# A two-layer fp32 transformer block on one core: the software-pipelined step order written anew

## The chip, the cores and the metric

One NeuronCore of one Trainium2 chip runs the kernel. TensorE (PE in the views) multiplies and transposes, VectorE (DVE), ScalarE (ACT) and GpSimd (POOL) work elementwise, SyncE (SP) issues the transfers. The metric is device time in microseconds of one launch.

## The reference, cut to what matters

The input x has 32 batches of 256 rows by 128 columns. Two layers follow each other; each adds an attention and a feed-forward part, both computed from the layer-normalised x.

```python
xn = layernorm(x)
# layer 0: cosine attention + (softmax attention + top-2 of 8 experts)
cos    = clip(l2norm(Q) @ l2norm(K), -0.999, 0.999)      # 16 heads of 8
W      = (1 - arccos(cos) / pi) ** 16
x = x + (W / (sum(W) + 1e-6)) @ V @ Wo + bo
      + softmax(q @ k / sqrt(8)) @ v + sum_top2(gate * (xn @ W_expert + b))
xn = layernorm(x)
# layer 1: causal attention (one head of 128) + FP4 gated MLP (width 352)
x = x + softmax(causal(q1 @ k1 / sqrt(128))) @ v1 @ w_out
      + fp4_linear(silu(fp4_linear(xn, w_gate)) * fp4_linear(xn, w_up), w_down)
```

`fp4_linear` rounds both operands to a grid of 4-bit values in blocks of 16.

## The kernel before, in words

All work on one batch (256 rows, two tiles of 128 partitions) is cut into about 150 small stages, each named by a pair (stage, argument). The list `SCHEDULE` at line 53 holds each of them once, with a lag. Step t of the program walks through the list and runs each stage on batch t + lag, so one step has work of four batches in it: lag 1 (the next batch's layer norm, projections, gate, stacking), lag 0 (scores), lag -1 (power, values, end of layer 0, start of layer 1) and lag -2 (end of the MLP). Steps t = -1 to 33 are run; 28 of them in a hardware loop of two steps a turn. Every engine walks through the same list and issues, in this order, only its own part of each stage. There is no planner at run time: an engine waits on semaphores for its inputs and for buffers, and everything behind a waiting instruction waits too.

The stages that the prediction speaks of, with what they issue in a step:

- `c` (8): PE makes the cosines of two heads in `psS`; DVE clips them into `curve` (L852). `sq` (4): POOL squares 2048 columns of `curve` into `root` (L500). `ln` (4): ACT logarithm of `root`. `sigm` (4): ACT sigmoid of `root`. `mul` (4): `curve` times `root`, arguments 0 and 2 on POOL (L503), 1 and 3 on DVE (L848). `arctan`, `wln`, `wexp` (4 each): ACT on `curve`. `pvw` (8): PE, values under these weights (L1199). `oC`, `oF`: ACT copies the sums out of `psV`; `finc`, `finf`: PE transposes them, DVE divides (L876 to L887).
- `m` (8): PE scores, DVE row maxima (L858). `maxT`: DVE splits the maxima, PE transposes, ACT copies `mT`. `e` (8): PE scores less the maxima, ACT exponentials `prob`. `pvf` (8): PE, values.
- `xnT`: DVE normalises, PE transposes, ACT copies `xnT`. `proj` (2): PE projects (L1004), ACT copies cosine q, k, v, DVE copies the softmax ones and the gate's (L769 to L774). `norm`: ACT squares, DVE sums (L779). `guess`: ACT, first guess of the inverse norms. `newton`: DVE refines them into `rn` (L791 to L793). `unit`: POOL multiplies q and k by `rn` (L514). `high` (4): ACT, high halves into `stk`; arguments 0 and 1 are the softmax k and q, 2 and 3 the cosine ones, which wait for `unit`. `stack` (4): POOL, low halves (L520). `stackT` (4): PE transposes, DVE copies (L844). `choose` (6), `gmax`, `gexp`: gate.
- `wo`, `ln1`, `rstd1`, `xn1T`, `quantx` (9 DVE steps of FP4 rounding), `p1`, `s1`, `s1e`, `p1T`, `o1`, `w1` (DVE L940), `xqT`, `gu` (2, PE L1167, ACT sigmoid `h`), `hmul` (2, DVE L946 and L948), `quanth` (9 DVE steps on 128x704, L409 to L425), `hT`, `down`: layer 1. `fadd`: POOL. `table` (2): ACT loads a table of functions (L563, L636).

Two lists are derived from `SCHEDULE`: `MISC` gives all small PE products their places in two PSUM banks in turn, `SCORES` does so for `c`, `m`, `e` in two slots of `psS`. A PE product waits until the one before it in its bank or slot has been read. So an order changes also which stage waits for which buffer. SP's queue has only `load` (lag 1) and `down`'s store (lag -2).

```python
for stage, arg, lag in SCHEDULE:
    if not isinstance(t, int) or 0 <= t + lag < B:
        run(stage, arg, t + lag, (parity + lag) % 2, t)
```

```python
if kind < 2:                       # high, on ACT
    act.wait_ge(s_stkq, due(s_stkq, b))
```

Of the kernel before, what the change touches and what calls it, by code (L numbers as in the profile page):

```python
# [1225 lines left out]
```

## Time and profile before

| what | value |
|---|---|
| median of 3 runs | 2045.9 us (2045.52 to 2048.73) |
| profiled execution, own time | 2050.03 us |
| its span | 2048.2 us |
| ACT busy | 1875.9 us (92%) |
| DVE busy | 1790.3 us (87%) |
| PE busy | 1625.1 us (79%) |
| POOL busy | 1062.5 us (52%) |
| mean granted TensorE clock | 0.924 |
| DMA | 11.21 MB, mean 5 GB/s |

Busy is the time in which at least one instruction of the engine ran. Instructions of one engine overlap a little at their ends, so the distance from one start to the next (below called pitch) can be shorter than a duration. A wait is shown in brackets behind a row of the timeline as the idle time and the instruction that ended it.

### The profile page before, as it was taken

How to read it: one execution, taken by the hardware profiler on the slowest of the kernel's cores; microseconds unless marked ns; L12 is line 12 of the kernel's file. 1: busy time of each engine (PE TensorE's matmuls, PEld its weight loads, DVE VectorE, ACT ScalarE, POOL GpSimd, SP SyncE). 2: the span in 40 equal slices, each digit the busy share in tenths (PEclk: the TensorE clock that was granted, in tenths of full speed). 3: DMA queues.
4: the chain of work that ended last, by engine and by line, in shares of the span. 5: the costliest groups of instructions: out<-in, count | busy, mean ns of one | idle time of the engine just before them, and what ended most of it. 6: DMA issues, size and time to landing. Idle time of an engine off the chain costs nothing.

```text
span 2048.2 us, 39684 instructions
## 1 busy us (share of the span) xinstructions
PE 1625.1 (79%) x12405; PEld 796.0 (39%) x12405; DVE 1790.3 (87%) x4071; ACT 1875.9 (92%) x2144; POOL 1062.5 (52%) x448
## 2 busy tenths in 40 slices
PE   2678788888888888888888888888888888887865
PEld 1233444433444443344444334444433444443433
DVE  5778989999998999999899999989999998998844
ACT  2399999999999999999999999999999999999991
POOL 1455555456555545655554565555456555545520
PEclk9979999999999999999999999999999999999875
DMA  1000000000000000000000000000000000000000
GB/s 41 4 4 1 6 6 0 5 6 5 6 5 6 0 5 6 5 6 5 6 0 5 6 5 6 5 6 0 5 6 5 6 5 6 0 5 7 4 4 6
DMA packets 21059, 11.21 MB, mean 5 GB/s; under 512 B 1431, under 2 KB 20953, under 8 KB 20956
## 3 DMA queue, kind: packets, MB, share of 16 engines
q1 hardware_dynamic: 20956, 10.20, 1.7%
q14 instruction: 83, 0.68, 0.1%
q8 instruction: 20, 0.33, 0.1%
...
## 4 chain that ended last, share of the span: by engine, by line
ACT 40%; DVE 23%; issue 22%; PE 13%; POOL 1%; DVEq 1%; ACTq 1%; SPq 0%; DMA 0%; POOLq 0%
ACT curve L532 21%; ACT root L532 7%; ACT prob L532 3%; PE psM L1167 3%; DVE nmax L858 3%; DVE curve L848 3%; PE psM L1004 2%; ACT L563 2%; ACT L636 1%; PE psV L1199 1%; DVE h L421 1%; ACT hqT L532 1%; POOL qk L514 1%; PE psM L1151 1%; DVE hqT L417 1%
## 5 line engine op out<-in xcount | busy, mean ns | idle before, releaser
L532 ACT ACTIVATE curve<-curve 128x2048 f32<-128x2048 f32 x384 | 717.7, 1902 | 4.8 <-POOL curve L503 3.4
L500 POOL TENSOR_TENSOR root<-curve 128x2048 f32<-128x2048 f32 x128 | 460.1, 3600 | 426.1 <-DVE curve L852 425.9
L532 ACT ACTIVATE root<-root 128x2048 f32<-128x2048 f32 x256 | 484.4, 1905 | 8.1 <-POOL root L500 7.8
L503 POOL TENSOR_TENSOR curve<-curve,root 128x2048 f32<-128x2048 f32 x64 | 348.8, 5452 | 93.3 <-ACT root L532 93.3
L852 DVE TENSOR_SCALAR curve<-psS 128x1024 f32<-128x1024 f32 x256 | 306.0, 1216 | 25.3 <-PE psS L1035 19.1
L858 DVE TENSOR_REDUCE nmax<-psS 128x4 f32<-128x1024 f32 x256 | 308.8, 1214 | 7.2 <-PE psS L1044 6.9
L1199 PE MATMUL psV<-prob,vf 128*32 128x256 f32 x2048 | 270.8, 425 | 3.9 <-ACT prob L532 0.6
L532 ACT ACTIVATE prob<-psS 128x1024 f32<-128x1024 f32 x256 | 261.3, 1021 | 11.8 <-PE psS L1065 11.0
L1199 PE MATMUL psV<-curve,vc 128*32 128x256 f32 x2048 | 225.4, 408 | 40.0 <-ACT curve L532 36.3
L520 POOL TENSOR_TENSOR stk<-qk,stk 128x512 f16<-128x512 f32 x128 | 168.4, 1325 | 155.3 <-ACT stk L532 155.3
L848 DVE TENSOR_TENSOR curve<-curve,root 128x2048 f32<-128x2048 f32 x64 | 177.7, 2777 | 5.6 <-ACT root L532 5.6
L832 DVE SCALAR_TENSOR_TENSOR acc<-psM,comb,acc 128x128 f32<-128x128 f32 x512 | 142.1, 344 | 27.0 <-PE psM L1012 25.4
L1167 PE MATMUL psM<-wguT,xqT 128*128 128x352 f32 x256 | 126.6, 623 | 42.0 <-ACT xqT L532 23.0
L1199 PEld LDWEIGHTS psV<-curve,vc 128*32 128x32 f32 x2048 | 96.4, 114 | 144.4 <-issue 111.1
L1012 PE MATMUL psM<-we,xnT 128*128 128x512 f32 x256 | 151.2, 674 | 0.0
L1199 PEld LDWEIGHTS psV<-prob,vf 128*32 128x32 f32 x2048 | 94.9, 118 | 141.8 <-issue 75.9
L1063 PE MATMUL psS<-stkT 32*128 32x256 f16 x1024 | 129.6, 276 | 2.0 <-ACT prob L532 1.6
L1065 PE MATMUL psS<-mT,onesb 32*128 32x256 bf16 x1024 | 127.3, 271 | 0.0
L1044 PE MATMUL psS<-stkT 32*128 32x256 f16 x1024 | 108.8, 294 | 3.5 <-DVE nmax L858 2.4
L1023 PE MATMUL psM<-ident,stk 128*128 128x128 f16 x1024 | 76.7, 225 | 36.9 <-DVE stkT L844 32.0
L514 POOL TENSOR_TENSOR qk<-qk,rn 128x512 f32<-128x512 f32 x32 | 34.4, 1073 | 136.3 <-DVE rn L793 136.3
L1035 PE MATMUL psS<-stkT 32*128 32x256 f16 x1024 | 83.7, 292 | 20.1 <-DVE curve L852 15.1
...
## 6 DMA issues: line engine op xcount, KB each, us to landing
...
```

Source lines behind the costliest of these rows:

```text
L500: nc.gpsimd.tensor_tensor(root[:, two], curve[:, p, two], curve[:, p, two], ALU.mult).then_inc(s_sq, 1)
L503: nc.gpsimd.tensor_tensor(curve[:, p, two], curve[:, p, two], root[:, two], ALU.mult).then_inc(s_half[0], 1)
L520: nc.gpsimd.tensor_tensor(lo, src, hi, ALU.subtract).then_inc(s_stk, 1)
L532: return nc.scalar.activation(out, in_, func, **kw)
L832: nc.vector.scalar_tensor_tensor(acc[:, p, j, :], bank[:, (e % 4) * D:(e % 4 + 1) * D], comb[:, p, j, e:e + 1], acc[:, p, j, :], ALU.mult, ...
L848: nc.vector.tensor_tensor(curve[:, p, two], curve[:, p, two], root[:, two], ALU.mult).then_inc(s_half[1], 1)
L852: nc.vector.tensor_scalar(curve[:, p, arg * UC:(arg + 1) * UC], psS[:, slot_of(stage, arg), :, :, :].rearrange("p a k q -> p (a k q)"), CO ...
L858: nc.vector.tensor_reduce(nmax[:, :, 2 * arg:2 * arg + 2].rearrange("p j a -> p a j"), psS[:, slot_of(stage, arg), :, :, :], AX.X, ALU.max ...
L1012: mm(bank[:, :], xnT[:, j * P:(j + 1) * P], we[:, 4 * arg:4 * arg + 4, :].rearrange("p e f -> p (e f)"), start=False, stop=True).then_inc( ...
L1063: mm(psS[:, slot, a, kt, :], stkT[rows(hh), 3, g, kt * P:(kt + 1) * P], stkT[rows(hh), 2, g, :], start=True, stop=False)
L1167: ins = mm(bank[:, 0:I], xqT[:, arg * P:(arg + 1) * P], wguT[:, m, :], start=True, stop=True)
L1199: ins = mm(psV[rows(hh), kind, half, :], head_window(v, p, kt, head_at(g, hh)), w[:, a, kt, :], start=(g % 2 == 0 and kt == 0), stop=(g % ...
```

## The change

Only the list `SCHEDULE` is replaced, by one with the same stages in another order; every instruction is the same. Some lags differ: `c` 1, 2 and 3 and `sq` 0 move from lag 0 to lag 1, `m` 3 from 1 to 0, `o1` from -2 to -1, `hmul` 1 from -1 to -2 (that is, over the boundary of a step). The core of it:

```diff
-    ("table", 0, -1), ("wln", 0, -1), ("c", 1, 0), ("sq", 0, 0), ("fadd", 0, -1), ("pvf", 7, -1), ("oF", 0, -1),
...
-    ("ln", 0, 0), ("m", 6, 0), ("experts", 1, 0), ("pvw", 3, -1), ("sq", 1, 0), ("sq", 2, 0), ("m", 7, 0),
-    ("pvw", 4, -1), ("sq", 3, 0), ("rstd0", 0, 1), ("stack", 0, 1), ("pvw", 5, -1), ("quanth", 1, -2), ("load", 0, 1),
-    ("unit", 0, 1), ("ln", 1, 0), ("oC", 0, -1), ("pvw", 6, -1), ("pvw", 7, -1), ("xnT", 0, 1), ("maxT", 0, 0),
-    ("quanth", 2, -2), ("quanth", 3, -2), ("c", 6, 0), ("c", 7, 0), ("proj", 0, 1), ("finc", 0, -1), ("stack", 1, 1),
-    ("ln", 2, 0), ("e", 0, 0), ("proj", 1, 1), ("norm", 0, 1), ("ocT", 0, -1), ("e", 1, 0), ("high", 0, 1),
-    ("w1", 0, -2), ("wo", 0, -1), ("stack", 2, 1), ("e", 2, 0), ("pvf", 0, 0), ("pvf", 1, 0), ("pvf", 2, 0),
-    ("ln1", 0, -1), ("ln", 3, 0), ("quanth", 4, -2), ("rstd1", 0, -1), ("xn1T", 0, -1), ("guess", 0, 1),
-    ("gexp", 0, 1), ("quantx", 0, -1), ("quanth", 5, -2), ("gmax", 0, 1), ("stack", 3, 1), ("quanth", 6, -2),
-    ("newton", 0, 1), ("e", 3, 0), ("quantx", 1, -1), ("choose", 0, 1), ("p1", 0, -1), ("high", 1, 1), ("e", 4, 0),
-    ("high", 2, 1), ("quanth", 7, -2), ("s1", 0, -1), ("choose", 1, 1), ("e", 5, 0), ("quantx", 2, -1), ("pvf", 3, 0),
-    ("s1e", 0, -1), ("e", 6, 0), ("high", 3, 1), ("quanth", 8, -2), ("quantx", 3, -1), ("residual", 0, 1),
...
-    ("pvf", 6, 0), ("down", 0, -2), ("mul", 2, 0), ("arctan", 1, 0), ("p1T", 0, -1), ("choose", 4, 1), ("mul", 3, 0),
-    ("arctan", 2, 0), ("gu", 1, -1), ("arctan", 3, 0), ("choose", 5, 1), ("hmul", 1, -1),
+    ("table", 0, -1), ("c", 4, 0), ("hmul", 1, -2), ("pvf", 7, -1), ("wln", 0, -1), ("wexp", 0, -1), ("m", 3, 0),
+    ("wln", 1, -1), ("ln0", 0, 1), ("wln", 2, -1), ("sq", 1, 0), ("quanth", 0, -2), ("wexp", 1, -1), ("c", 5, 0),
...
+    ("w1", 0, -2), ("pvw", 3, -1), ("m", 7, 0), ("rstd0", 0, 1), ("ln", 0, 0), ("ln", 1, 0), ("pvw", 4, -1),
+    ("sq", 2, 0), ("pvw", 5, -1), ("pvw", 6, -1), ("xnT", 0, 1), ("maxT", 0, 0), ("pvw", 7, -1), ("oC", 0, -1),
+    ("c", 7, 0), ("proj", 0, 1), ("oF", 0, -1), ("sq", 3, 0), ("finc", 0, -1), ("finf", 0, -1), ("ln", 2, 0),
+    ("e", 0, 0), ("quanth", 3, -2), ("proj", 1, 1), ("norm", 0, 1), ("ocT", 0, -1), ("e", 1, 0), ("gmax", 0, 1),
+    ("e", 2, 0), ("quanth", 4, -2), ("wo", 0, -1), ("guess", 0, 1), ("high", 0, 1), ("quanth", 5, -2), ("ln1", 0, -1),
+    ("pvf", 0, 0), ("fadd", 0, -1), ("unit", 0, 1), ("load", 0, 1), ("e", 3, 0), ("quanth", 6, -2), ("pvf", 1, 0),
+    ("e", 4, 0), ("rstd1", 0, -1), ("high", 1, 1), ("pvf", 2, 0), ("e", 5, 0), ("xn1T", 0, -1), ("pvf", 3, 0),
+    ("quanth", 7, -2), ("quantx", 0, -1), ("quantx", 1, -1), ("quanth", 8, -2), ("quantx", 2, -1), ("newton", 0, 1),
+    ("gexp", 0, 1), ("stack", 0, 1), ("e", 6, 0), ("quantx", 3, -1), ("choose", 0, 1), ("quantx", 4, -1),
+    ("p1", 0, -1), ("stack", 1, 1), ("s1", 0, -1), ("choose", 1, 1), ("high", 2, 1), ("quantx", 5, -1), ("pvf", 4, 0),
+    ("stackT", 0, 1), ("choose", 2, 1), ("ln", 3, 0), ("s1e", 0, -1), ("e", 7, 0), ("quantx", 6, -1),
...
+    ("sigm", 1, 0), ("hT", 1, -2), ("xqT", 0, -1), ("sigm", 2, 0), ("c", 0, 1), ("mul", 0, 0), ("choose", 5, 1),
+    ("mul", 1, 0), ("mul", 2, 0), ("rs1", 0, -1), ("gu", 0, -1), ("sigm", 3, 0), ("sq", 0, 1), ("hmul", 0, -1),
+    ("pvf", 6, 0), ("c", 1, 1), ("down", 0, -2), ("c", 2, 1), ("arctan", 0, 0), ("arctan", 1, 0), ("o1", 0, -1),
+    ("arctan", 2, 0), ("gu", 1, -1), ("mul", 3, 0), ("arctan", 3, 0), ("c", 3, 1),
```

## Rows read from the trace of the kernel before

**Rows 1.** Busy us (xcount) of PE, PEld, DVE, ACT, POOL, granted clock, DMA: 300 to 900.

```profile
300.00:900.00 600.00, 494.70 (x3888) 243.29 (x3886) 553.40 (x1256) 585.39 (x664) 332.45 (x131) 0.95 0.02 5
```

**Rows 2.** The instructions of line 563, the table load that opens a step on ACT.

```profile
L563 ACT ACT_TABLE_LOAD  x32: 1283/1283/1283, 127.4 to 1981.7; - x32
```

**Rows 3.** Timeline of ACT over one period, from the middle of the run.

```profile
1013.37 0.46 ACT L532 ACTIVATE h<-psM 128x352 f32<-128x352 f32 x1 [1.00 <-PE psM L1167]
...
1024.87 1.91 ACT L532 ACTIVATE curve<-curve 128x2048 f32<-128x2048 f32 x1
1026.69 0.58 ACT L532 ACTIVATE oFs<-psV 128x512 f32<-128x512 f32 x1
...
1043.96 0.58 ACT L532 ACTIVATE oCs<-psV 128x512 f32<-128x512 f32 x1
1044.44 0.37 ACT L532 ACTIVATE xnT<-psM 128x256 f32<-128x256 f32 x1
...
1048.12 1.03 ACT L532 ACTIVATE prob<-psS 128x1024 f32<-128x1024 f32 x1
1049.02 0.40 ACT L532 ACTIVATE qk<-psM 128x256 f32<-128x256 f32 x1
...
1059.38 0.64 ACT L532 ACTIVATE stk<-qk 128x512 f16<-128x512 f32 x1
...
1104.33 0.37 ACT L532 ACTIVATE xnT<-psM 128x256 f32<-128x256 f32 x1
```

**Rows 4.** Timeline of DVE over the same period.

```profile
1011.50 2.88 DVE L848 TENSOR_TENSOR curve<-curve,root 128x2048 f32<-128x2048 f32 x1
...
1030.63 0.34 DVE L885 RECIPROCAL rsF<-psM 128x32 f32<-128x32 f32 x1
1031.02 0.42 DVE L887 TENSOR_TENSOR of<-psM,rsF 128x256 f32<-128x256 f32 x1
...
1047.07 0.41 DVE L769 TENSOR_TENSOR qk<-psM,wfb 128x256 f32<-128x256 f32 x1
...
1048.27 0.42 DVE L880 TENSOR_TENSOR oc<-psM,rsC 128x256 f32<-128x256 f32 x1
1049.71 0.42 DVE L769 TENSOR_TENSOR qk<-psM,wfb 128x256 f32<-128x256 f32 x1 [1.02 <-PE psM L1004]
...
1051.30 0.61 DVE L940 SCALAR_TENSOR_TENSOR x<-psM,rs,x 128x128 f32<-128x128 f32 x2
...
1057.54 0.23 DVE L793 SCALAR_TENSOR_TENSOR rn<-rnt,rn 128x64 f32<-128x64 f32 x1
```

**Rows 5.** The instructions of six lines; durations in ns, least, median, longest.

```profile
L417 DVE TENSOR_SCALAR hqT<-h x32: 494/718/726, 215.8 to 2034.4; 128x704 uint32<-128x704 uint32 x32
L423 DVE SCALAR_TENSOR_TENSOR h<-hqT,h x32: 882/1440/1444, 220.9 to 2036.4; 128x704 f32<-128x704 f32 x32
L425 DVE TENSOR_TENSOR h<-h,qa x32: 826/1359/1368, 223.9 to 2037.4; 128x704 f32<-128x704 f32 x32
L848 DVE TENSOR_TENSOR curve<-curve,root x64: 2276/2885/4499, 115.3 to 1975.6; 128x2048 f32<-128x2048 f32 x64
L503 POOL TENSOR_TENSOR curve<-curve,root x64: 4524/5441/6610, 112.1 to 1970.5; 128x2048 f32<-128x2048 f32 x64
L500 POOL TENSOR_TENSOR root<-curve x128: 3593/3600/3605, 67.8 to 1945.0; 128x2048 f32<-128x2048 f32 x128
```

**Rows 6.** Timeline of POOL over the same period.

```profile
1012.44 6.37 POOL L503 TENSOR_TENSOR curve<-curve,root 128x2048 f32<-128x2048 f32 x1 [0.20 <-ACT root L532]
...
1057.92 1.07 POOL L514 TENSOR_TENSOR qk<-qk,rn 128x512 f32<-128x512 f32 x1 [4.40 <-DVE rn L793]
```

**Rows 7.** Timeline of PE over the same period.

```profile
1010.62 2.71 PE L1167 MATMUL psM<-wguT,xqT 128*128 128x352 f32 x4 [0.30 <-ACT xqT L532]
...
1048.75 0.93 PE L1004 MATMUL psM<-wf,xnT 128*128 128x392 f32 x2
```

**Rows 8.** The view of rows 1 for 1010 to 1015 us.

```profile
1010.00:1015.00 5.00, 4.70 (x16) 1.73 (x12) 4.70 (x5) 4.00 (x6) 4.79 (x2) 0.50 0.00 0
```

More of the change, by code:

```diff
@@ L69 @@
-    ("quantx", 4, -1), ("choose", 2, 1), ("pvf", 4, 0), ("e", 7, 0), ("quantx", 5, -1), ("table", 1, 0),
-    ("stackT", 0, 1), ("stackT", 1, 1), ("sigm", 0, 0), ("quantx", 6, -1), ("stackT", 2, 1), ("quantx", 7, -1),
-    ("hT", 0, -2), ("choose", 3, 1), ("sigm", 1, 0), ("quantx", 8, -1), ("m", 0, 1), ("stackT", 3, 1), ("mul", 0, 0),
-    ("m", 1, 1), ("hT", 1, -2), ("xqT", 0, -1), ("m", 2, 1), ("mul", 1, 0), ("sigm", 2, 0), ("gu", 0, -1),
-    ("pvf", 5, 0), ("hmul", 0, -1), ("rs1", 0, -1), ("m", 3, 1), ("arctan", 0, 0), ("sigm", 3, 0), ("c", 0, 1),
@@ L74 @@
-    ("pvf", 6, 0), ("down", 0, -2), ("mul", 2, 0), ("arctan", 1, 0), ("p1T", 0, -1), ("choose", 4, 1), ("mul", 3, 0),
-    ("arctan", 2, 0), ("gu", 1, -1), ("arctan", 3, 0), ("choose", 5, 1), ("hmul", 1, -1),
+    ("table", 0, -1), ("c", 4, 0), ("hmul", 1, -2), ("pvf", 7, -1), ("wln", 0, -1), ("wexp", 0, -1), ("m", 3, 0),
+    ("wln", 1, -1), ("ln0", 0, 1), ("wln", 2, -1), ("sq", 1, 0), ("quanth", 0, -2), ("wexp", 1, -1), ("c", 5, 0),
+    ("quanth", 1, -2), ("wln", 3, -1), ("experts", 0, 0), ("m", 4, 0), ("pvw", 0, -1), ("wexp", 2, -1), ("m", 5, 0),
@@ new lines @@
+    ("experts", 1, 0), ("pvw", 1, -1), ("quanth", 2, -2), ("pvw", 2, -1), ("wexp", 3, -1), ("m", 6, 0), ("c", 6, 0),
+    ("w1", 0, -2), ("pvw", 3, -1), ("m", 7, 0), ("rstd0", 0, 1), ("ln", 0, 0), ("ln", 1, 0), ("pvw", 4, -1),
+    ("sq", 2, 0), ("pvw", 5, -1), ("pvw", 6, -1), ("xnT", 0, 1), ("maxT", 0, 0), ("pvw", 7, -1), ("oC", 0, -1),
+    ("c", 7, 0), ("proj", 0, 1), ("oF", 0, -1), ("sq", 3, 0), ("finc", 0, -1), ("finf", 0, -1), ("ln", 2, 0),
+    ("e", 0, 0), ("quanth", 3, -2), ("proj", 1, 1), ("norm", 0, 1), ("ocT", 0, -1), ("e", 1, 0), ("gmax", 0, 1),
@@ new lines @@
+    ("p1", 0, -1), ("stack", 1, 1), ("s1", 0, -1), ("choose", 1, 1), ("high", 2, 1), ("quantx", 5, -1), ("pvf", 4, 0),
+    ("stackT", 0, 1), ("choose", 2, 1), ("ln", 3, 0), ("s1e", 0, -1), ("e", 7, 0), ("quantx", 6, -1),
+    ("residual", 0, 1), ("table", 1, 0), ("choose", 3, 1), ("stack", 2, 1), ("high", 3, 1), ("quantx", 7, -1),
+    ("pvf", 5, 0), ("quantx", 8, -1), ("stackT", 1, 1), ("choose", 4, 1), ("stackT", 2, 1), ("sigm", 0, 0),
+    ("m", 0, 1), ("m", 1, 1), ("hT", 0, -2), ("stack", 3, 1), ("p1T", 0, -1), ("stackT", 3, 1), ("m", 2, 1),
```

3 lines of the change are left out of this document (removed).

## The prediction

> **What bounds the kernel now.** I read first the busy time by stretch: in the long middle of the run ACT is busy for 585.4 of 600 us and DVE for 553.4 [rows 1]. A reordering takes no work away, so at most the 2.4% in which ACT rests are there to be won, and a new wait of ACT costs its full length, since ACT has almost nothing to make it up with. Then the table loads: a step opens with one, 32 of them from 127.4 to 1981.7 us, so a period is 1854.3 / 31 = 59.8 us [rows 2], ahead of it lie 127 us of filling and behind it 66 us of draining. Third the timeline of ACT over one period: its instructions follow each other at 1.82 us for 2048 columns (1024.87 to 1026.69) and 0.90 for `prob` (1048.12 to 1049.02), with one clear wait of 1.00 us, for the first product of `gu` [rows 3].
>
> I cut a period at two points of ACT: X, the start of the copy `xnT` (1044.44), and H, the start of `high` 2 (1059.38), the first that needs `unit`. From X to H it is 14.94 us now, from H to the next X (1104.33) 44.95 [rows 3]. Both stretches hold in the new order too, and a circle runs through them: X lets PE project, DVE copies, finishes the norms, POOL multiplies, and only then may ACT do H; from H on ACT works in order until X. The period can't be shorter than this circle.
>
> **The change, from H to X.** By the two lists, ACT has two `e`, `oC` and `oF` less in this stretch than now and one `ln` more: -2 x 0.90 - 2 x 0.48 (1043.96 to 1044.44) + 1.82 = -0.94 us [rows 3]. `wexp` 0 now stands right behind `wln` 0, whose output it reads, so it can't begin before that one has ended: 1.91 in place of 1.82, some +0.1 [rows 3]. The wait at `gu` 0 stays: again only `sigm` 2 stands between the copy `xqT` and it, and the products take 2.71 us at a granted clock of 0.50 [rows 7, 8]. I follow the other inputs by their places: mul 2, mul 3, `hT`, `stackT`, the `wexp` for `pvw` come out in time, some by less than 1 us. So 44.95 - 0.94 + 0.1 = 44.1 us.
>
> The moved lags cost nothing of their own: `c` 1 to 3 and `sq` 0 are the same work a little sooner, `hmul` 1 finds its input (`gu` 1) ready because `mul` 3, `c` 3 and `c` 4 (some 4.5 us of DVE) stand between, and `o1` is copied out of PSUM in ACT's order a step sooner, beside `p1T` as before. SP's queue has the same two stages; `load` 0 passes no store, and the input is needed a whole step later. If that cover were gone, `ln0` would be late first, and it has 12 us to X.
>
> **From X to H.** ACT's own work here grows by two `e`, `oC` and `oF` less one `ln`, to about 14.6 us of pitches [rows 3], but DVE is longer, and it is behind the same X:
>
> - X to the second `proj` on DVE: 5.27 us now (1044.44 to 1049.71), with `finc` between the two [rows 3, 4]. Now `finf` is there too, and since both copies leave the same two banks, the last product of `proj` 1 must wait until DVE has read `finf`. X to the first copy 2.63, copy and `finc` 1.62 (1047.07 to 1048.69), `finf` 0.81 (1030.63 to 1031.44), the product 0.93, two handovers of 0.05: 6.1 [rows 4, 7]. `quanth` 3 lies in the shadow of that product, but may begin late (below): I take 6.3.
> - From there to the end of `newton`: 8.06 us now (1049.71 to 1057.77) [rows 4]. `w1` goes away, 0.61 and its wait of 0.1 [rows 4]. `quanth` 7 and 8 and `quantx` 1 and 2 come in ahead of it. `quanth` 7 and 8 have a median of 1.44 and 1.36, but a least of 0.88 and 0.83 [rows 5]. The difference is a wait for POOL: now they run beside POOL's `unit` and `stack`. In the new order `unit` waits for `newton`, which is behind them, and nothing else is left for POOL, so I take the least: 1.71, less 0.1 of overlap. For the same reason `quanth` 4 goes from 0.72 to 0.49 [rows 5]. The two small ones are 0.3. Sum: 8.06 - 0.7 + 1.6 - 0.2 + 0.3 = 9.1.
> - `newton` to the end of `unit`: 1.22 us now (1057.77 to 1058.99) [rows 4, 6]. `quantx` 3, with two inputs in SBUF, comes directly behind `newton` and is ahead of `unit` by the 0.15 that the semaphore takes; I add 0.2.
>
> 6.3 + 9.1 + 1.4 = 16.8 us, against 14.94. ACT stands before `high` 2 (and a little before `ln1`, which is also behind more DVE work) and loses what it now has in small waits and more. DVE in turn has rested before `proj` 0.
>
> **The sum.** 16.8 + 44.1 = 60.9 us a period against 59.8: +1.1. A period pays this when it has both lag 1 and lag -2 work, t = 2 to 30, so 29 times: +32 us. The filling and draining chains hold the same steps; I see 1 or 2 us either way and take zero. The profiled execution's own 2050.0 us becomes 2082, and the median, 4.1 lower, 2045.9 + 32 = 2078 us.
>
> **A row and a rule.** DVE's `mul` at 1011.50 took 2.88 us where the least is 2.28, and POOL's `mul` began at 1012.44, took 6.37, where the least is 4.52 [rows 4 to 6]. That is 0.6 of DVE waiting, until POOL's previous `mul` ended, and then 1.9 of POOL waiting, until DVE's ended at 1014.38: 1012.44 + 1.94 + 4.43 = 1018.81. They don't share, they take turns. The Trainium skill says so on the page SBUF — State Buffer, section "SBUF: two separate sides": whichever of the two starts first holds the shared pair of ports for its whole instruction, and the other blocks. The trace agrees with it by these numbers.
>
> **The rivals.**
>
> *A, the turn lost (slower still).* In the new order POOL has `sq` 0 directly behind `mul` 2, and DVE comes to `mul` 3 at about H + 18.7, while by the same durations `mul` 2 ends at H + 19.5, having waited for `mul` 1 [rows 5]. If DVE is there first it goes ahead of `sq` 0 and ends at 21.8, in time for `arctan` 3 at 22.1. If it comes over 0.8 us later, `sq` holds the ports for 3.60 us [rows 5] and `arctan` 3 is late by about 3.3 us: +4.4 a period, +128 us, 2174; in some periods only, by that share. By the rule of the Trainium skill, SBUF — State Buffer, section "Who interferes with whom", each such miss costs the whole rest of the other instruction; the forecast's sum has the good turn.
>
> *B, the clock moves.* The products of `gu` 0 ran at half clock and those of the circle, `proj`, `finc`, `finf`, `e`, did not [rows 7, 8]. With PE's pauses elsewhere, the half clock can fall on the circle: two products of the 0.93 kind lie on it [rows 7], so half the clock costs about 1 us, as much as at `gu` 0, +2.1 a period, +61 us: 2107.
>
> *C, the other side: faster.* The half clock leaves `gu` 0 and doesn't come to the circle: up to the 1.00 us of that wait is gone [rows 3]. With the short end of the circle too (6.0, 8.9 and 1.22: 16.1) a period is 59.2, -0.6: -17 us, 2029. It decides against the forecast from the point where the circle is shorter than 15.7 us with the wait at its present size, or 16.7 without it. For it speaks only that the clock moved in and out in the old order too; against, that DVE's added steps are there in the list.
>
> *D, nothing shows.* `quanth` and the rest lie in DVE's slack (46.6 us in 600) [rows 1] and the wait before `high` 2 only takes the place of the small ones that ACT has now: period as before, 2046. This needs the two errors of C at half size.
>
> **How the numbers follow.** Forecast 0.50 (a period longer by 0.4 to 1.9), A 0.12, B 0.12, C 0.16, D 0.10. That leaves a measured difference under 0.2% (4 us, about what a measurement of this kernel can tell from none) to D: faster 0.16, same 0.10, slower 0.74. For the range: the low end takes C's half, a period of -0.3 us: 2037; the high end must take B's whole and the costs at which I took the least: `quanth` 7 and 8 at their medians are +1.1 a period, +32 over the forecast, 2110, and a few turns lost on top, 2118.
>
> **What the profile would show.** Right: the two table loads of a period about 60.9 us apart; ACT with a wait of 1 to 2 us before a `stk` instruction, ended by POOL L514, in nearly every period; POOL L514 with a wait for DVE L793 longer than now; L423 and L425 on `h` near 0.88 and 0.83; DVE resting before L769. A: a wait of ACT before a `curve` activation, ended by DVE L848, of about 3 us, and L848 over 5 us. B: L1004 and L1080 longer, PEclk 0.50 in their stretch. C: no wait of `h` for L1167 and a wait before `stk` below 1 us. The prediction is wrong at its root if ACT waits nowhere for L514: then I mistook which engine is last at H. It is wrong in size if the stretch from H to X isn't near 44.1, which would mean a wait that I passed over when I followed the places.

## The result

The changed kernel takes 2094.95 us (median of 4, 2090.68 to 2098.91), the one before 2047.32 (4 runs, 2045.52 to 2050.22): ratio 1.0227, 95% interval 1.0214 to 1.0239, so 47.6 us slower. 2078 was predicted, with a range of 2037 to 2118. The direction and the place are right; 15.6 us of the loss are missing.

Two lines of the page of the changed kernel, the busy time and the granted clock in 40 slices. ACT's work is the same as before, its share lower; the granted clock is under 0.9 in more slices, its mean is 0.876 where it was 0.924.

```profile
span 2093.7 us, 39627 instructions
PE 1728.5 (83%) x12405; PEld 830.3 (40%) x12405; DVE 1778.0 (85%) x4071; ACT 1882.2 (90%) x2144; POOL 1122.6 (54%) x448
...
PEclk9678889989889898888998888998988998988976
```

The view of [rows 1], and the table loads of [rows 2], now of the changed kernel. In the middle ACT is busy for 571.5 of 600 us instead of 585.4. The loads lie 1904.7 / 31 = 61.44 us apart instead of 59.82: 1904.7 - 1854.3 = +50.4 over the 31 periods. Less 2.2 ahead of the first and 2.7 behind the last (63.8 us instead of 66.5), this makes 45.5, and the two profiled executions differ by 45.5 (2095.52 and 2050.03).

```profile
300.00:900.00 600.00, 518.53 (x3783) 248.66 (x3779) 531.45 (x1224) 571.49 (x643) 338.59 (x125) 0.89 0.02 5
```

```profile
L563 ACT ACT_TABLE_LOAD  x32: 1283/1283/1283, 125.2 to 2029.9; - x32
```

The timeline of ACT over one ordinary period (compare [rows 3]). X is at 1004.85, H at 1021.70, the next X at 1065.83: 16.85 and 44.13 us, where 16.8 and 44.1 were forecast. (That the first agrees so well is luck in part, see below.)

```profile
1004.85 0.36 ACT L532 ACTIVATE xnT<-psM 128x256 f32<-128x256 f32 x1
1007.15 0.38 ACT L532 ACTIVATE qk<-psM 128x256 f32<-128x256 f32 x1 [0.55 <-PE psM L1004]
...
1021.70 0.63 ACT L532 ACTIVATE stk<-qk 128x512 f16<-128x512 f32 x1 [0.17 <-POOL qk L514]
...
1035.94 0.46 ACT L532 ACTIVATE h<-psM 128x352 f32<-128x352 f32 x1 [1.01 <-PE psM L1167]
...
1046.04 1.28 ACT L563 ACT_TABLE_LOAD   x1
...
1065.83 0.36 ACT L532 ACTIVATE xnT<-psM 128x256 f32<-128x256 f32 x1
```

DVE and POOL in the same period (compare [rows 4, 6]). The second projection's copy on DVE is at X + 7.04, `newton` ends 8.46 later (1020.35), `unit` ends 1.28 after that (1021.63): the circle. L423 and L425 (`quanth` 7 and 8) take 0.88 each.

```profile
1007.81 0.42 DVE L769 TENSOR_TENSOR qk<-psM,wfb 128x256 f32<-128x256 f32 x1 [0.27 <-PE psM L1004]
...
1010.20 1.77 DVE L415 SCALAR_TENSOR_TENSOR h<-h,qr 128x704 f32<-128x704 f32 x1
1011.89 0.41 DVE L769 TENSOR_TENSOR qk<-psM,wfb 128x256 f32<-128x256 f32 x1
...
1017.38 0.88 DVE L423 SCALAR_TENSOR_TENSOR h<-hqT,h 128x704 f32<-128x704 f32 x1
...
1018.71 0.88 DVE L425 TENSOR_TENSOR h<-h,qa 128x704 f32<-128x704 f32 x1
...
1020.13 0.22 DVE L793 SCALAR_TENSOR_TENSOR rn<-rnt,rn 128x64 f32<-128x64 f32 x1
...
1041.08 2.38 DVE L848 TENSOR_TENSOR curve<-curve,root 128x2048 f32<-128x2048 f32 x1
```

```profile
1007.62 3.60 POOL L500 TENSOR_TENSOR root<-curve 128x2048 f32<-128x2048 f32 x1 [14.34 <-DVE curve L852]
...
1020.52 1.11 POOL L514 TENSOR_TENSOR qk<-qk,rn 128x512 f32<-128x512 f32 x1 [7.96 <-DVE rn L793]
...
1035.01 6.30 POOL L503 TENSOR_TENSOR curve<-curve,root 128x2048 f32<-128x2048 f32 x1 [0.74 <-ACT root L532]
```

But not all periods are like this one. These are means over the same 25 periods of each trace (X number 5 to 29 to the next X), read off the timelines of ACT:

| kernel | X to H | H to X | period |
|---|---|---|---|
| before | 14.94 | 44.80 | 59.74 |
| changed | 17.22 | 44.23 | 61.44 |

In the changed kernel every fifth period from X = 818.61 on has 19.4 us from X to H. Here is PE's timeline just behind that X, and the window view there. The clock is 0.72, the products of the maxima and of `pvw` 7 are late (1.01 and 1.92 us, where they take 0.61 and 1.06 at X = 1004.85, at a clock of 1.00), and `curve` on DVE, ahead of the projection's copy, waited 3.60 us (2.11 in an ordinary period, at most 1.3 before). The projection's own products run at full clock (0.91).

```profile
819.15 1.01 PE L1055 MATMUL psM<-identb,mstk 128*128 128x128 bf16 x8 [0.65 <-DVE mstk L868]
820.09 1.92 PE L1199 MATMUL psV<-curve,vc 128*32 128x256 f32 x8
821.94 0.53 PE L1035 MATMUL psS<-stkT 32*128 32x256 f16 x4
822.40 0.91 PE L1004 MATMUL psM<-w0T,xnT 128*128 128x384 f32 x2
```

```profile
818.00:824.00 6.00, 5.29 (x27) 2.39 (x27) 2.12 (x6) 2.99 (x7) 0.09 (x1) 0.72 0.00 0
```

Two of DVE's waits for TensorE between 300 and 1800 us have grown, from 14.3 to 70.1 and from 12.2 to 42.6 us. Most of the first belongs to the order itself: DVE now comes to the clip of `c` 7 with nothing else to do and waits 2.11 us for its product in ordinary periods too. The second, for the experts' products, is the one that goes when the clock is up again (10.0 us in experiment 10, where the first is still 62.4):

```profile
DVE curve L852 <- PE psS L1035: 70.1, 46, 3.7
...
DVE acc L832 <- PE psM L1012: 42.6, 54, 2.0
```

This second wait also reaches ordinary periods. Rows of DVE and PE ahead of X = 1004.85: the experts' product takes 2.08 us, DVE waits for it, and so it ends its split of the maxima (L868) at 1004.21, 0.64 before X. In experiment 10 it ends 1.23 before X (997.52, X = 998.75), and the projection, whose products take the same time in both, comes 0.59 sooner behind X. The same holds period by period, in the 25 of the changed kernel and the 25 of experiment 10: where DVE waits 0.2 or 0.7 us for the experts in the 25 us ahead of X, the second projection's copy comes at X + 6.4; where it waits 1.5 to 1.8, at X + 6.9 to 7.1; where it waits 2.4 to 3.2, at X + 8.2 to 9.7.

```profile
990.87 1.90 DVE L832 SCALAR_TENSOR_TENSOR acc<-psM,comb,acc 128x128 f32<-128x128 f32 x7 [0.99 <-PE psM L1012]
...
1003.91 0.30 DVE L868 TENSOR_TENSOR mstk<-nres,mstk 128x32 bf16<-128x32 f32 x1
```

```profile
988.75 2.08 PE L1012 MATMUL psM<-we,xnT 128*128 128x512 f32 x2
```

### The profile page after: what moved, and what is told of

Same layout as the page of the kernel before. It is cut to its first block, busy times and chain, and to the rows that moved or that the text cites. A ratio compares the mean times of both kernels' runs of the same rounds, so it can differ in the third digit from the quotient of the medians.

```text
span 2093.7 us, 39627 instructions
## 1 busy us (share of the span) xinstructions
PE 1728.5 (83%) x12405; PEld 830.3 (40%) x12405; DVE 1778.0 (85%) x4071; ACT 1882.2 (90%) x2144; POOL 1122.6 (54%) x448
## 4 chain that ended last, share of the span: by engine, by line
DVE 32%; PE 31%; ACT 17%; issue 16%; POOL 2%; DVEq 1%; SPq 0%; ACTq 0%; DMA 0%; POOLq 0%
PE psM L1012 8%; PE psV L1199 6%; ACT curve L532 5%; ACT root L532 4%; DVE curve L852 4%; PE psM L1167 4%; DVE curve L848 3%; DVE nmax L858 3%; PE psM L1004 2%; PE psM L1011 2%; ACT L636 2%; DVE h L415 2%; PE psS L1044 2%; ACT prob L532 2%; PE psS L1035 2%
## 5 line engine op out<-in xcount | busy, mean ns | idle before, releaser
L500 POOL TENSOR_TENSOR root<-curve 128x2048 f32<-128x2048 f32 x128 | 523.1, 4097 | 482.0 <-DVE curve L852 480.3
L1199 PE MATMUL psV<-prob,vf 128*32 128x256 f32 x2048 | 286.7, 403 | 0.0
L532 ACT ACTIVATE prob<-psS 128x1024 f32<-128x1024 f32 x256 | 254.6, 1020 | 13.7 <-PE psS L1065 9.0
L1199 PE MATMUL psV<-curve,vc 128*32 128x256 f32 x2048 | 237.6, 413 | 29.4 <-ACT curve L532 22.5
L1012 PE MATMUL psM<-we,xnT 128*128 128x512 f32 x256 | 206.0, 898 | 1.2 <-issue 1.2
L514 POOL TENSOR_TENSOR qk<-qk,rn 128x512 f32<-128x512 f32 x32 | 35.5, 1108 | 285.9 <-DVE rn L793 285.9
L520 POOL TENSOR_TENSOR stk<-qk,stk 128x512 f16<-128x512 f32 x128 | 149.9, 1181 | 71.0 <-ACT stk L532 71.0
L848 DVE TENSOR_TENSOR curve<-curve,root 128x2048 f32<-128x2048 f32 x64 | 162.7, 2542 | 6.2 <-ACT root L532 6.2
L1167 PE MATMUL psM<-wguT,xqT 128*128 128x352 f32 x256 | 132.9, 636 | 38.5 <-ACT o1T L532 33.3
L1023 PE MATMUL psM<-ident,stk 128*128 128x128 f16 x1024 | 84.0, 237 | 37.8 <-ACT hqT L532 28.7
L1065 PE MATMUL psS<-mT,onesb 32*128 32x256 bf16 x1024 | 112.4, 268 | 0.0
```

What stands on the lines that cost most here:

```text
L500: nc.gpsimd.tensor_tensor(root[:, two], curve[:, p, two], curve[:, p, two], ALU.mult).then_inc(s_sq, 1)
L520: nc.gpsimd.tensor_tensor(lo, src, hi, ALU.subtract).then_inc(s_stk, 1)
L532: return nc.scalar.activation(out, in_, func, **kw)
L848: nc.vector.tensor_tensor(curve[:, p, two], curve[:, p, two], root[:, two], ALU.mult).then_inc(s_half[1], 1)
L1012: mm(bank[:, :], xnT[:, j * P:(j + 1) * P], we[:, 4 * arg:4 * arg + 4, :].rearrange("p e f -> p (e f)"), start=False, stop=True).then_inc( ...
L1167: ins = mm(bank[:, 0:I], xqT[:, arg * P:(arg + 1) * P], wguT[:, m, :], start=True, stop=True)
```

## The experiments

Two theories. *Circle*: the new order puts `quanth` 7 and 8 and `quantx` 1 and 2 ahead of `newton`, and a period is as long as the way X, projection, DVE, `newton`, `unit`, H and ACT's work back to X. *Clock*: the loss, or what of it the circle doesn't give, comes from TensorE being granted half its clock (1.2 in place of 2.4 GHz) in other places. List edits are shown cut to the entries that move. Three kernels add products that change no value; this is said where they come.

**1. Undo the late `newton` alone**, in the changed kernel.

```diff
     ("xn1T", 0, -1),
+    ("newton", 0, 1),
     ("pvf", 3, 0), ("quanth", 7, -2), ("quantx", 0, -1), ("quantx", 1, -1), ("quanth", 8, -2), ("quantx", 2, -1),
-    ("newton", 0, 1),
```

> The changed order with one stage moved back: newton directly behind xn1T, so ahead of quanth 7, quantx 0 and 1, quanth 8 and quantx 2. Nothing that TensorE does moves. Circle theory (DVE's work ahead of newton makes ScalarE wait at high 2): newton ends 2.3 us sooner, ScalarE's own work becomes last in the stretch from xnT to high 2, which falls from 16.9 to about 15.6 us, while quanth 7 and 8 grow from 0.88 to about 1.4 us beside GpSimd, where nobody waits for them: period 61.4 to about 60.1, time about 2057 us (2045 to 2065). Rival, half clock: the periods whose proj runs at half clock carry the loss, DVE's order does not; then the time stays within 10 us of 2095. Rival, banks: the products of proj 1 waiting for finf's bank carry it; then it stays near 2095 too.

2156.72 us, ratio 1.0535 [1.0514, 1.0555]: slower still. At best, X to H fell to 15.98, no further: there `unit` had ended 1.59 us before H (X = 1029.69, `unit` at 1044.08, H at 1045.67), so this is ACT's own way from X to H in the new order, its small waits included. H to X rose from 44.2 to 45.2 or more in most periods, since ACT's exponential of layer 1 now waits for DVE's maxima (17.2 us in 23 waits between 300 and 1800), and to 47.5 to 49.5 in nine of the periods, where a turn is lost. The row of ACT at this H, then rows of DVE, POOL and ACT in a period with a lost turn: DVE's `mul` 3 came at 1128.54, 0.86 after POOL's `mul` 2 had ended at 1127.68, and by then POOL had begun the square (1127.63). The square took its 3.60, DVE's instruction ended at 1133.38, and ACT's arctangent had stood for 2.52.

```profile
1045.67 0.62 ACT L532 ACTIVATE stk<-qk 128x512 f16<-128x512 f32 x1
```

```profile
1128.54 4.84 DVE L848 TENSOR_TENSOR curve<-curve,root 128x2048 f32<-128x2048 f32 x1
```

```profile
1121.61 6.07 POOL L503 TENSOR_TENSOR curve<-curve,root 128x2048 f32<-128x2048 f32 x1 [0.57 <-ACT root L532]
1127.63 3.60 POOL L500 TENSOR_TENSOR root<-curve 128x2048 f32<-128x2048 f32 x1
```

```profile
1133.41 1.91 ACT L532 ACTIVATE curve<-curve 128x2048 f32<-128x2048 f32 x1 [2.52 <-DVE curve L848]
```

So the new order is tight in more than one place, and undoing an edit doesn't price it. In the changed kernel itself `mul` 3 began at 1041.08, 0.23 before `mul` 2 ended (1041.31), and went ahead of the square: it took 2.38. So rival A, a lost turn, was close: DVE was there 0.23 us before `mul` 2 ended. In the profiled execution no turn was lost between 300 and 1800 us (no L848 of over 3 us; the longest, 4.34, began at 118 us, in the filling phase).

**2. Do the DVE part alone**: the order of before, with `quanth` 7 and 8 ahead of `newton`.

```diff
+    ("quanth", 7, -2), ("quanth", 8, -2),
     ("newton", 0, 1), ("e", 3, 0), ("quantx", 1, -1), ("choose", 0, 1), ("p1", 0, -1), ("high", 1, 1), ("e", 4, 0),
     ("high", 2, 1),
-    ("quanth", 7, -2),
...
-    ("quanth", 8, -2),
```

> The old order with quanth 7 and quanth 8 moved ahead of newton, all else as before. Circle theory: newton ends 1.6 us later (0.81 and 0.75 uncontended), the slack of 0.4 us before high 2 is used up, xnT to high 2 goes from 14.94 to about 16.1 us; period 59.8 to 61.0, time about 2047 + 34 = 2081 us (2070 to 2090). Rival, DVE's slack hides it (both steps become about 0.55 us shorter since they no longer meet GpSimd): 2047, within 4 us. Half clock or banks theory: 2047 as well, since TensorE's order is the old one.

2094.71 us, 1.0225 [1.0209, 1.0241]: two stages moved on DVE cost as much as the whole change. X to H is 16.48 in every period of the table below (14.94 before), H to X 44.96, and the mean clock is 0.94 in the middle as before. ACT, DVE and POOL of one period (this kernel's source is one line longer, so L423 is L424 here): `newton` ends 1.82 later after X, POOL follows at once, and ACT stands 1.41. The view puts that down to "issue", yet it ends 0.08 after POOL's multiplication, which ended at 1022.24.

```profile
1022.32 0.63 ACT L533 ACTIVATE stk<-qk 128x512 f16<-128x512 f32 x1 [1.41 <-issue]
```

```profile
1018.53 0.89 DVE L424 SCALAR_TENSOR_TENSOR h<-hqT,h 128x704 f32<-128x704 f32 x1
1019.45 0.89 DVE L426 TENSOR_TENSOR h<-h,qa 128x704 f32<-128x704 f32 x1
...
1020.77 0.23 DVE L794 SCALAR_TENSOR_TENSOR rn<-rnt,rn 128x64 f32<-128x64 f32 x1
```

```profile
1021.16 1.08 POOL L515 TENSOR_TENSOR qk<-qk,rn 128x512 f32<-128x512 f32 x1 [6.23 <-DVE rn L794]
```

X here is 1005.85, so `newton` ends at X + 15.15, as against X + 13.33 before. This shows the circle by itself: 1.8 us more of DVE, about 0.3 of it free, 1.7 a period lost with what little H to X adds; 29 of them would be 49 us, 45.6 were measured.

**3. `quanth` 3 behind the second projection**, in the changed kernel. It waits there for POOL's square (1.77 us instead of its least 0.88).

```diff
-    ("quanth", 3, -2), ("proj", 1, 1), ("norm", 0, 1),
+    ("proj", 1, 1), ("norm", 0, 1), ("quanth", 3, -2),
```

> The changed order with quanth 3 moved from ahead of proj 1 to behind norm; nothing else. In the changed kernel its first instruction on h takes 1.77 us where 0.88 is the least, since GpSimd squares at that time, and the second proj waits behind it on DVE. Turn-taking theory: proj 1 on DVE comes 0.8 us sooner, quanth 3 then costs 0.8 undisturbed, so xnT to high 2 falls by 0.5 to 0.9 us: time about 2095 - 20 = 2075 us (2068 to 2082). Rival: it only meets GpSimd's fadd instead and proj 1 waits for its product anyway: less than 0.2 us a period, 2090 to 2095.

2099.93 us, 1.0254 [1.0238, 1.027]. X to H was 16.6 to 17.3 in the 25 periods, and the ones with 19.4 were gone, yet the mean period is the same 61.45. Its place wasn't what made the circle long. Where the clock is full in both kernels, the second projection's copy comes at X + 5.86 here and at X + 6.44 with `quanth` 3 ahead of it; but behind the projection the stage adds 0.95 to the way to `newton` (9.40 instead of 8.45). Ahead of it it costs 0.6 us and hides 0.4; behind it nothing is hidden, and X to H is 17.2 in most periods where it was 16.85.

**4. ACT's wait for `gu` 0**, in the order of before: `sigm` 3 ahead of `gu` 0, so that ACT has 1.9 us more to do while PE multiplies at half clock.

```diff
-    ("gu", 0, -1), ("pvf", 5, 0), ("hmul", 0, -1), ("rs1", 0, -1), ("m", 3, 1), ("arctan", 0, 0), ("sigm", 3, 0),
+    ("sigm", 3, 0), ("gu", 0, -1), ("pvf", 5, 0), ("hmul", 0, -1), ("rs1", 0, -1), ("m", 3, 1), ("arctan", 0, 0),
```

> The old order with sigm 3 moved ahead of gu 0, so that two sigmoids of ScalarE stand between the copy xqT and the sigmoid of gu 0 and not one; TensorE's order is untouched. In the kernel before this wait is 1.00 us in two periods of three. Theory that ScalarE is last everywhere else in the stretch from high 2 to xnT: the wait goes, the stretch falls from 44.8 to about 44.1, time about 2047 - 22 = 2025 us (2018 to 2032). Rival: hmul 0, mul 1 and mul 2 come later on DVE and GpSimd relative to ScalarE and arctan waits for them by as much: 2043 to 2050.

2049.25 us, 0.9998 [0.9988, 1.0009]. The wait (19.3 us in the middle) is gone, and nothing is gained. The first three of ACT's waits between 300 and 1800 us, in this kernel; the rows of before read 5.6 for `prob`, 0.9 for `qk`, and none for `p1T`:

```profile
ACT p1T L532 <- PE psM L1134: 10.3, 12, 1.2
ACT prob L532 <- PE psS L1065: 6.9, 29, 0.3
ACT qk L532 <- PE psM L1004: 6.4, 23, 0.9
```

**5. The same with `p1T` moved out of the way** (behind `hT` 0).

```diff
     ("hT", 0, -2),
+    ("p1T", 0, -1),
...
-    ("p1T", 0, -1),
```

> The old order with sigm 3 ahead of gu 0, as in the run that changed nothing, and p1T moved from behind arctan 1 to behind hT 0, since in that run the wait for p1T (10.3 us in 1500) had taken over part of the one for gu 0 (19.3). If a wait on ScalarE is only worth what the next one leaves of it, both gone give 0.5 us a period: 2047 - 15 = 2032 us. Rival: the bank of the next product is now the bound and the time stays at 2047, within 4 us.

2058.25 us, 1.0033 [1.0008, 1.0058], with a wide spread (2048.0 to 2071.2) and a clock of 0.898. Now `curve` waits for POOL (11.2 us), `prob` for PE (10.2), `qk` for PE (8.9), and X to H is 16.0 to 16.4 in eleven of 29 periods; in ten of them products of the projection took 0.7 to 1.0 us instead of 0.5 to 0.6 (half clock), as in experiment 12 below.

**6. `newton` early and `mul` 3 early**, in the changed kernel: experiment 1 with its lost turn mended, `mul` 3 moved ahead of `c` 2.

```diff
-    ("pvf", 6, 0), ("c", 1, 1), ("down", 0, -2), ("c", 2, 1), ("arctan", 0, 0), ("arctan", 1, 0), ("o1", 0, -1),
-    ("arctan", 2, 0), ("gu", 1, -1), ("mul", 3, 0), ("arctan", 3, 0), ("c", 3, 1),
+    ("pvf", 6, 0), ("c", 1, 1), ("down", 0, -2), ("mul", 3, 0), ("c", 2, 1), ("arctan", 0, 0), ("arctan", 1, 0),
+    ("o1", 0, -1), ("arctan", 2, 0), ("gu", 1, -1), ("arctan", 3, 0), ("c", 3, 1),
```

> The kernel with newton early (2157 us, period 61 to 65) with mul 3 moved ahead of c 2 on DVE as well. In ten of its periods ScalarE waited 2.4 us on average for VectorE's mul 3, whose longest took 5.69 us: it came after sq 0 had started on GpSimd. Turn theory: one clip (1.13 us) earlier, mul 3 is always there before sq 0; its longest is under 4.6 us, no wait of arctan for L848 is left, and the time falls by 24 us at least, to about 2130. Rival: the order of the two engines at the ports is drawn anew each time and does not hang on who came first; then waits for L848 stay and the time is within 10 us of 2157.

2171.34 us, 1.0578 [1.0539, 1.0617], clock 0.852. No wait of ACT for L848 is left among its larger ones (0.2 us in all), so the turns are right, and still it is the second slowest of all. Its loss is TensorE: one window behind a step's start, and an experts' product in it.

```profile
1087.00:1095.00 8.00, 7.98 (x23) 2.02 (x23) 6.78 (x18) 7.94 (x7) 6.19 (x2) 0.50 0.00 1
```

```profile
1087.55 2.08 PE L1012 MATMUL psM<-we,xnT 128*128 128x512 f32 x2
```

PE is busy for 7.98 of 8 us at 0.50, the product takes 2.08 where it takes 1.12 at 1.00, and what follows (`pvw`, `xnT`, the maxima) is late: ACT waits 28.0 us for `xnT` and 16.9 for `mT`. X to H jumps between 16.0, 17.7 and 19.1, H to X is 47.7 every other time.

**7. And `quanth` 7 and 8 behind `s1`**, so that layer 1's maxima come sooner.

```diff
     ("p1", 0, -1), ("stack", 1, 1), ("s1", 0, -1),
+    ("quanth", 7, -2), ("quanth", 8, -2),
```

> The same with quanth 7 and quanth 8 moved behind s1 too, as they are in the old order, so that DVE's s1 comes 1.7 us sooner and ScalarE's s1e no longer waits for it (0.8 us a period with newton early). With the circle cut to ScalarE's own 16.0 us and high 2 to xnT at 44.3 a period is 60.3: time about 2060 us (2050 to 2080, the upper part where the half clock falls on proj in some periods). Rival: the stages that come after (quantx 5 to 8, stackT) are only pushed back and the stretch from high 2 to xnT stays at 45.3: 2095 or more.

2199.58 us, 1.0717 [1.068, 1.0754], clock 0.85. The wait for the maxima is no longer among ACT's larger ones, but `xnT` waits 42.9 us and `mT` 24.3: as in 6, and more.

**8. `oF` and `finf` at the start of a step**, where they were before, in the changed kernel: it takes `finf` (0.81 us of DVE) from the circle.

```diff
     ("pvf", 7, -1),
+    ("oF", 0, -1),
...
     ("pvw", 0, -1),
+    ("finf", 0, -1),
...
-    ("oF", 0, -1), ("sq", 3, 0), ("finc", 0, -1), ("finf", 0, -1),
+    ("sq", 3, 0), ("finc", 0, -1),
```

> The changed order with oF and finf moved back to the start of the step, where the old order has them. Bank theory, my term of 0.81 us: the last product of proj 1 need no longer wait until VectorE has read finf, and VectorE has one stage less between xnT and newton; xnT to high 2 falls from 16.9 to about 16.1, time about 2095 - 22 = 2073 us. Rival: quanth 3 is then in the way instead, behind GpSimd's squaring, and proj 1 starts as late as now: 2090 to 2097.

2109.33 us, 1.0289 [1.0234, 1.0344]. X to H is 16.3 at best but mostly 16.8 to 18.0, as `ln1`'s logarithm waits for DVE (16.3 us in 22 waits) and `qk` for PE (11.5). The 0.81 us of `finf` are not won even at best. This is DVE behind X = 1198.10, one of the best periods: `quanth` 3 begins sooner, waits for the same square of POOL (1200.27 to 1203.87), takes 2.51 us instead of 1.77, and the second projection's copy comes at X + 6.44, as with `finf` in place (6.45 in experiment 10). So the mechanism of the rival was right: this copy was held up by the square and `quanth` 3 behind it, not by `finf` and its bank.

```profile
1202.11 2.51 DVE L415 SCALAR_TENSOR_TENSOR h<-h,qr 128x704 f32<-128x704 f32 x1
1204.54 0.41 DVE L769 TENSOR_TENSOR qk<-psM,wfb 128x256 f32<-128x256 f32 x1
```

**9 and 10. Fill PE's rests.** In the changed kernel PE rests 0.89, 0.34, 0.67 and 0.60 us between 1041 and 1047, and the experts behind them run at half clock for a part (up to 1.98 us for two products that take 1.12). Both kernels add work that changes no value: the first product of `gu` 1 is made three times, and `pvf` 7 gets eight products with weights of zero, 1.9 us of PE in a period. Number 9 does it to the kernel of 6, number 10 to the changed kernel.

```diff
-    ins = mm(bank[:, 0:I], xqT[:, arg * P:(arg + 1) * P], wguT[:, m, :], start=True, stop=True)
+    for again in range(3 if (arg, m) == (1, 0) else 1):
+        ins = mm(bank[:, 0:I], xqT[:, arg * P:(arg + 1) * P], wguT[:, m, :], start=True, stop=True)
...
+for again in range(2 if v is vf and u == 7 else 0):
+    for kt in range(NT):
+        for a in range(2):
+            hh = 2 * (u % 2) + a
+            mm(psV[rows(hh), kind, half, :], causal[:, 1, 0:FULL_GROUP], w[:, a, kt, :],
+               start=False, stop=False, tile_position=(0, FULL_GROUP * hh))
```

> The kernel with newton and mul 3 early (2171 us) plus work for TensorE that changes no value, put where it pauses around the start of a step: the first product of gu 1 is made three times, and pvf 7 gets eight more products with zero weights (1.06 us). In that kernel TensorE's granted clock falls to 0.50 for up to 14 us behind those pauses, the products of experts take 2.08 us in place of 1.12 and xnT comes late. Clock theory: with the pauses filled these stretches become shorter or go, high 2 to xnT falls back from 47.7 to about 45.2 in the bad periods, and the time falls by at least 30 us, to 2140 or less. Rival: TensorE's own work is what is late; 1.9 us more of it makes the same periods longer still, 2171 or more.

2130.96 us, 1.0417 [1.0398, 1.0435], clock 0.907: 40 us faster than the kernel of 6 by more work.

> The changed kernel with the same added work (gu 1's first product three times, eight products with zero weights in pvf 7). In it one period of five has its proj at half clock, 19.4 us from xnT to high 2 in place of 16.9, behind a stretch of 10 us at half clock. Clock theory: with the pauses filled these periods go and all are 61.2 us, time about 2095 - 7 = 2088 us; the other four fifths, which the circle through DVE sets, don't move. Rival: no pattern changes, 2095 within 3 us, or the added work is late and it is above 2100.

2060.48 us, 1.0062 [1.0048, 1.0076], clock 0.937: 34.5 us faster than the changed kernel, much more than I expected. (The projection itself, which I had thought at half clock in every fifth period, is at full clock in all of them in the changed kernel; it only begins late.) Windows ahead of the experts and on them, first of the changed kernel (X = 1004.85), then of this one (X = 998.75, so the same places), then two rows of this one's PE and one of its DVE:

```profile
1036.00:1046.00 10.00, 8.10 (x62) 4.09 (x60) 9.53 (x11) 10.00 (x8) 10.00 (x2) 0.93 0.09 27
1046.00:1054.00 8.00, 7.22 (x29) 1.98 (x25) 7.47 (x20) 7.91 (x8) 7.89 (x3) 0.79 0.00 1
```

```profile
1029.90:1039.90 10.00, 10.00 (x80) 5.59 (x76) 9.51 (x12) 9.98 (x8) 10.00 (x2) 0.96 0.09 27
1039.90:1047.90 8.00, 6.49 (x29) 2.15 (x28) 7.96 (x20) 7.92 (x7) 7.51 (x3) 1.00 0.00 1
```

```profile
1036.59 1.92 PE L1201 MATMUL psV<-prob,causal 128*32 128x256 f32 x16
...
1040.42 1.12 PE L1012 MATMUL psM<-we,xnT 128*128 128x512 f32 x2
```

```profile
997.22 0.30 DVE L868 TENSOR_TENSOR mstk<-nres,mstk 128x32 bf16<-128x32 f32 x1
```

With PE busy throughout, the clock stays at 1.00 over the experts and the products that follow are on time. X to H is now 16.26 nearly everywhere, and between filling and draining none of 19.4 is left. Its three parts in this period: 6.45, 8.47 and 1.26 us. Filling doesn't mean full clock everywhere: the mean between 300 and 1800 us is 0.96 (0.89 in the changed kernel, 0.94 before).

**11. `quanth` 7 alone ahead of `newton`**, in the order of before: half the dose of 2.

```diff
+    ("quanth", 7, -2),
     ("newton", 0, 1), ("e", 3, 0),
...
-    ("quanth", 7, -2),
```

> The old order with quanth 7 alone moved ahead of newton. With quanth 7 and 8 moved, newton came 1.78 us later and high 2 1.54 later in each period. Circle theory with the slack of 0.39 us that the trace of before shows (unit ends at 1058.99, high 2 begins at 1059.38): 0.92 later makes 0.5 to 0.6 us a period, time about 2047 + 17 = 2064 us (2058 to 2070). Rival, no slack: half of the 45 us, 2070 or more. Rival, the loss begins only with quanth 8: 2047.

2093.66 us, 1.0229 [1.0215, 1.0243], clock 0.903. I expected 2064. In its first periods X to H is 15.56, the 0.6 that half a dose gives; later it is 16.6 to 17.2 in most, and there the clock is half from X on. One such period, where the projection is late by 0.89 before ACT has read it once:

```profile
1003.02 0.38 ACT L533 ACTIVATE qk<-psM 128x256 f32<-128x256 f32 x1 [0.89 <-PE psM L1005]
```

```profile
1000.00:1004.00 4.00, 3.20 (x16) 1.48 (x14) 3.00 (x3) 3.11 (x7) 0.89 (x1) 0.65 0.00 0
```

The circle and the clock are not two rivals here: a shift of 0.6 us was followed by half clock on the projection, and together they are 1.6. That the shift moved PE's rests, and these the clock, is my reading and not shown by this run.

**12. Fill PE's rests in the order of before**, the control for 10. Work that changes no value is added again.

```diff
-    for qt_ in range(NT):
+    for again in range({0: 2, 1: 3}.get(arg, 1)):
+        for qt_ in range(NT):
...
     if stage == "o1":
+        pe.wait_ge(s_oC, due(s_oC, b))
+        for again in range(5):
+            mm(psV[:, 0, 0, :], ident[:, :], wfb[:, 0:T], start=True, stop=True)
```

> The order of before, with TensorE work added that changes no value: the products of the gathered half 0 made twice and of half 1 three times (behind them PE pauses 0.46 and 0.81 us), and in o1, while PE waits 2.15 us for its bank, five 128x128x256 products into the cosine sums' bank, which pvw 0 starts anew. Clock theory (time is lost where the clock is granted at half, and those stretches go when the pauses ahead of them are filled): the stretches at X+25..32 and X+44..48 go or shrink, the wait of ACT's h for the product of L1167 (1.00 us in two of three periods) shrinks, H to X falls from 44.8 to about 44.2, X to H stays 14.94, and the time falls from 2047 to about 2030 (2022 to 2040), faster than both kernels. Rival (ACT's chain from H to X is bound by other work just behind that wait, as in the run with sigm 3 ahead of gu 0, or the added products come late themselves): another wait takes the place, 2047 within 4 us, or slower.

2048.97 us against 2049.11, 0.9999 [0.999, 1.0008]: no gain, the rival was right. The clock did rise (0.98 in the middle, from 0.94), and `h` waits 13.3 us instead of 19.3. But X to H is 16.12 in every eighth period, since the clock is half on the projection there. Rows of ACT and PE and the window behind X = 984.49:

```profile
986.56 0.38 ACT L532 ACTIVATE qk<-psM 128x256 f32<-128x256 f32 x1 [0.79 <-PE psM L1004]
```

```profile
986.32 1.51 PE L1004 MATMUL psM<-wf,xnT 128*128 128x392 f32 x2
```

```profile
984.00:989.00 5.00, 4.00 (x16) 2.18 (x16) 3.24 (x6) 4.12 (x7) 2.55 (x1) 0.66 0.00 0
```

**All in one table** (means over 25 periods; the profiled execution of 10 was 11.6 us above its median, and most of its periods are 59.4 to 60.8):

| kernel | median | X to H | H to X | period |
|---|---|---|---|---|
| before | 2047.3 to 2049.2 | 14.94 | 44.80 | 59.74 |
| 12, before, filled | 2048.97 | 15.08 | 44.64 | 59.72 |
| 2, `quanth` 7, 8 first | 2094.71 | 16.48 | 44.96 | 61.44 |
| 11, `quanth` 7 first | 2093.66 | 16.53 | 44.78 | 61.31 |
| changed | 2094.95 | 17.22 | 44.23 | 61.44 |
| 10, changed, filled | 2060.48 | 16.36 | 44.01 | 60.37 |
| 1, `newton` early | 2156.72 | 17.08 | 46.15 | 63.23 |
| 6, and `mul` 3 early | 2171.34 | 17.64 | 46.31 | 63.94 |
| 9, 6 filled | 2130.96 | 17.13 | 45.29 | 62.42 |

No experiment beat the kernel before.

## Why the prediction was right, and where it was small

- *From X to H*: forecast 16.8, and 16.85 in the period shown, 17.22 on average. The mechanism is shown by experiment 2, where the clock is as before, and by the first periods of 11: DVE's extra work ahead of `newton` makes X to H longer, one for one after the first 0.3 us (1.82 makes 1.54, 0.93 makes 0.62). The forecast's parts were off in opposite directions. X to the second projection was taken as 6.3 and is 7.04; with the rests filled it is 6.45, and the other 0.6 is DVE's wait for the experts at half clock. `newton`'s part was taken as 9.1 and is 8.46 and 8.47. `unit`'s was 1.4 and is 1.28. So the forecast of 16.8 assumed full clock and was 0.5 too long for that (16.26); that it met the 16.85 of an ordinary period is luck.
- *The way to the second projection* was not the forecast one. `finf` and the product behind it would give X + 5.86 (experiment 3), where 6.1 was reckoned. POOL's square and `quanth` 3 behind it set the 6.45 (experiment 8); 0.2 had been allowed for them.
- *ACT's own work from X to H* was put at about 14.6 us. That was too small: in the 25 periods ACT is busy there for 15.5 us on average, where it was 14.4 before, and its own way, small waits included, is 15.98 (experiment 1). So the circle through DVE is longer than ACT's own way by only 0.3 us (16.26), and with `newton` early the forecast's 44.1 gives a period of 60.1, not 59.8.
- *`quanth` 7 and 8 at their least*: right, 0.88 each; POOL had nothing else to do. `quanth` 3 did begin late and take 1.77 beside POOL's square, as forecast, but it outlasted the projection's product by 0.6 us.
- *From H to X*: forecast 44.1, 44.13 in the period shown and 44.23 on average; `gu` 0's wait stayed at 1.01.
- *The sum*: the term "+1.1 a period" was mis-sized. It is +1.63 over the whole run (+1.70 in the 25 periods), and with PE's rests filled it is nearer +0.4: of 47.6 us, 12.6 stay in experiment 10 (12.6 / 31 = 0.4) and 35 go when PE gets 1.9 us more to do. Experiment 12, where the same kind of filling changes nothing in the old order, says that this is not something filling gives to any order. So +1.1 came near the measured +1.6 with two errors that partly cancel: the circle without the clock's part was put too long, and the clock's part was left out. Zero for filling and draining was off by 4.9 us in the other direction.
- *Rival B*, with 0.12, was priced at 2107 - 2078 = 29 us over the forecast, as a case that excludes it, with the projection's products at half clock. These products never were, between filling and draining. But the half clock did reach the circle by other products: by those of the maxima and `pvw` 7 just ahead of the projection in one period of five (2.5 us each time), and by the experts' in most others (0.6 us). On the projection itself it lay in experiments 11 and 12 (1.2 us in 12). The step that failed was to keep the clock of the old trace in the sum and to let it move only in a rival.
- *Rival A* was right about the mechanism and the 4.8 to 5.7 us that L848 takes when it is lost (experiment 1), and rightly not the forecast. But DVE was put 0.8 us ahead of the end of `mul` 2 and was 0.23 ahead in the period shown, so that it wasn't lost is luck in part. On this the trace bears out the Trainium skill, SBUF — State Buffer, section "Who interferes with whom": the instruction that comes second waits out the whole rest of the other (of the 4.84, 2.69 are the square's, up to 1131.23, and 2.15 its own).
- *Rivals C and D* fell: no period of the changed kernel has X to H under 16.2 behind the filling phase, against 14.94 before.
- *The sign in the profile* that I named, ACT standing 1 to 2 us before a `stk`, was wrong in size: it stands 0.2 us for L514 in nearly every period (4.4 us in 24). ACT's own work fills most of the stretch, and the rest of the loss is spread over earlier small waits for PE (`qk` 10.8 us, `mT` 6.0, `hqT` 4.4, `oCs` 3.2 in the middle). In experiment 2 it does stand in one piece of 1.4.

What stays open is why the clock falls where it does. Rests alone don't say it: just ahead of X = 1004.85 PE rested 0.69, 0.71 and 0.66 us and the clock stayed at 1.00; ahead of and behind X = 818.61 it rested 1.62 and 0.65 us, and the clock was 0.61 from 818 to 822 us. Filling worked in 9 and 10, raised the clock and gave nothing in 12, and in 11 a shift of 0.6 us went with half clock on the projection. That most of the 35 us go through the clock is what the rows of 10 say (two experts' products in 1.12 us, DVE's wait for them 10.0 us instead of 42.6, X to the projection longer or shorter with that wait, no period of 19.4); whether the added products also help by something else wasn't told apart.
